# Projection stages of an attention kernel: both operand stacks of a tile are made ahead of the returns of turned heads, and products stand between a batch's last turns

## What is computed

```python
xn = _rms_norm(x, g_norm) * (1.0 + scale) + shift
qkv = (xn @ W_qkv).reshape(b, n, 3, h, d)          # 16 heads of 32
q = _rms_norm(q, g_q)
k = _rms_norm(k, g_k)
logits = jnp.einsum('bhqd,bhkd->bhqk', q, k) * d ** (-0.5)
attn = jax.nn.softmax(logits, axis=-1)
o = jnp.einsum('bhqk,bhkd->bhqd', attn, v)
return o + o @ W_out                               # o with its heads side by side
```

## Time and profile before

| | us |
|---|---|
| median of 3 runs | 2251.61 |
| lowest, highest | 2249.65, 2253.29 |
| the profiled execution | 2247.79 |
| its span in the trace | 2246.0 |
| busy PE, DVE, ACT, POOL | 2129.1, 1630.1, 1293.8, 527.2 |
| projection stage of batch 0 (first product to first score) | 60.3 |
| the same of batch 1 | 64.8 |
| the same of batch 3 | 71.6 |
| from 745 us to the end: the GRU and what goes with it | 1501 |

### The profile page before, as it was taken

The page is one execution under the profiler, slowest core; times in us unless marked ns, Lnnn a source line. Parts: engine busy times, 40 slices in busy tenths (PEclk is TensorE's granted clock), DMA queues, the critical chain, the costliest instruction groups (busy, mean ns, idle before and its releaser), DMA issues.

```text
span 2246.0 us, 135671 instructions
## 1 busy us (share of the span) xinstructions
PE 2129.1 (95%) x57232; PEld 1830.8 (82%) x57232; DVE 1630.1 (73%) x6269; ACT 1293.8 (58%) x5763; POOL 527.2 (23%) x2255
## 2 busy tenths in 40 slices
PE   5768999999989999999999999999999999999998
PEld 3654555645545899999999999999999999999997
DVE  7987967878678487777677776667766666766665
ACT  6765947758568345555556655555555545555553
POOL 2002121021120222332233322222222222222221
PEclk8559999999999999999999999999999999999999
DMA  5000000010010000000000000000000000000000
GB/s 208 3 2 1 1 1 1 1 57 1 1 57 1 22 5 5 5 1 1 1 1 1 1 11 1 1 11 1 1 11 1 1 1 10 1 1 11 13 9 14
DMA packets 8410, 26.49 MB, mean 12 GB/s; under 512 B 1028, under 2 KB 1352, under 8 KB 7880
## 3 DMA queue, kind: packets, MB, share of 16 engines
q1 hardware_dynamic: 7712, 23.07, 2.8%
q10 hardware_dynamic: 424, 0.07, 0.0%
HBM read 18.94 MB, written 4.19 MB: 10 GB/s over the span
## 4 chain that ended last, share of the span: by engine, by line
PE 80%; DVE 12%; ACT 4%; issue 2%; DMA 1%; POOL 0%; SPq 0%; DVEq 0%; POOLq 0%; ACTq 0%
PE psum L2257 54%; PE psum L2218 8%; PE psum L2005 3%; PE psum L1926 3%; PE psum L1968 2%; PE psum L2023 2%; PE psum L2103 2%; PE psum L1989 2%; DVE region_cols L1232 2%; DVE region_cols L1248 2%; DVE top L1425 2%; ACT region_rows L786 1%; PE psum L1945 1%; DMA region_cols<-in_L_cond_W_emb_dram 1%; PE psum L1902 1%
## 5 line engine op out<-in xcount | busy, mean ns | idle before, releaser
L2257 PE MATMUL psum<-partsA,region_w_hh 128*128 128x40 f16 x24576 | 855.3, 179 | 10.4 <-issue 4.8
L2257 PE MATMUL psum<-partsB,region_w_hh 128*128 128x40 f16 x24576 | 853.3, 179 | 0.6 <-issue 0.5
L2257 PEld LDWEIGHTS psum<-partsA,region_w_hh 128*128 128x128 f16 x24576 | 758.7, 96 | 37.1 <-issue 11.2
L2257 PEld LDWEIGHTS psum<-partsB,region_w_hh 128*128 128x128 f16 x24576 | 724.1, 96 | 1.1 <-issue 0.5
L599 POOL TENSOR_TENSOR region_w_b<-region_w_b 128x16 f32<-128x16 f32 x1022 | 245.3, 240 | 1078.4 <-DVE region_w_b L1751 1078.4
L1725 DVE TENSOR_REDUCE psum<-psum 128x8 f32<-128x32 f32 x1024 | 201.7, 197 | 198.6 <-PE psum L2257 187.7
L1061 ACT ACTIVATE mixA<-psum 128x8 f32<-128x8 f32 x512 | 95.3, 186 | 428.3 <-DVE psum L1725 428.3
L1075 ACT ACTIVATE region_w_b<-psum 128x8 f32<-128x8 f32 x1024 | 190.0, 186 | 144.0 <-DVE psum L1740 86.9
L601 POOL COPY region_work<-region_w_b 128x8 f32<-128x8 f32 x1024 | 230.9, 225 | 2.2 <-DVE region_w_b L1751 2.2
L1751 DVE TENSOR_TENSOR_SCAN region_w_b<-giveB,region_w_b 128x40 f32<-128x40 f32 x512 | 123.8, 242 | 129.0 <-ACT region_w_b L1075 129.0
L1732 DVE TENSOR_REDUCE psum<-psum 128x8 f32<-128x32 f32 x1024 | 191.1, 187 | 0.7 <-PE psum L2257 0.6
(11 more groups left out here) (265 smaller groups left out, 2820.9 us busy)
## 6 DMA issues: line engine op xcount, KB each, us to landing
region_rows<-in_x_dram SPq DMA_DIRECT2D x4, 1024.0 KB, 11.1
region_w_a<-in_L_cond_W_qkv_dram SPq DMA_DIRECT2D x1, 3072.0 KB, 23.4
region_w_hh<-in_L_cond_W_hh_dram SPq DMA_DIRECT2D x4, 768.0 KB, 6.3
region_w_a<-in_L_cond_W_ih_dram SPq DMA_DIRECT2D x1, 3072.0 KB, 9.9
out_dram<-region_w_b SPq DMA_DIRECT2D x12, 256.0 KB, 2.2
region_cols<-in_L_cond_W_emb_dram SPq DMA_DIRECT2D x1, 2048.0 KB, 19.5
region_cond<-in_cond_dram SPq DMA_DIRECT2D x1, 1024.0 KB, 11.0
region_w_a<-in_L_cond_W_out_dram SPq DMA_DIRECT2D x1, 1024.0 KB, 21.5
```

Of the source, the lines that this page charges most:

```text
L2257: made = e.matmul(k.slots(bank)[:, :, ch, :, 0:2], k.w16[:, 2 * read + c, part, NC * "rzn".index(g) + 2 * half + ch], k.parts[read][:, c]. ...
```

## The change

On ACT and DVE the order within a tile is changed. Both stacks of tile t - 1 are made one after the other. Then the keys of tile t - 2 are returned, tile t is taken (squares, reduction, roots), and only then are the queries of tile t - 1 returned. On DVE the normalising now stands at the end of `dve_take_projected`, ahead of the values. At a batch's end, the return of tile 2's keys stands behind both stacks of tile 3. On PE the order of the projections stays. Only between the turns of tile 3's queries and keys there stand now two matmuls, of output product 3 or, in batch 0, of the last values, for which `pe_project` got an argument for the input chunks. In batches 1 to 3 the other two matmuls of product 3 stand one before the first and one before the second pair of scores.

```diff
 def act_attention
     for t in range(1, NT):
+        act_stack(e, k, b, t - 1, 0)
+        act_stack(e, k, b, t - 1, 1)
         if t > 1:
             act_turn_stack(e, k, b, t - 2, 1)
-        act_stack(e, k, b, t - 1, 0)
+        act_take_projected(e, k, b, t)
         act_turn_stack(e, k, b, t - 1, 0)
-        act_stack(e, k, b, t - 1, 1)
-        act_take_projected(e, k, b, t)
...
-    act_turn_stack(e, k, b, NT - 2, 1)
     act_stack(e, k, b, NT - 1, 0)
     act_stack(e, k, b, NT - 1, 1)
+    act_turn_stack(e, k, b, NT - 2, 1)
...
 def dve_take_projected
     e.tensor_reduce(k.head_power[:, t], k.sq_qk, AX.X, ALU.add).then_inc(s["head_power"], 1)
-    if values_in_turn(b, t):
-        dve_values(e, k, b, t)
...
     e.reciprocal(k.head_power[:, t], k.head_power[:, t]).then_inc(s["head_power"], 1)
+    dve_norm_heads(e, k, b, t)
+    if values_in_turn(b, t):
+        dve_values(e, k, b, t)
...
 def dve_attention
     for t in range(1, NT):
+        dve_stack(e, k, b, t - 1, 0)
+        dve_stack(e, k, b, t - 1, 1)
+        if b == 0 and t == 1:
+            dve_mask_taken(e, k, b + 1)
         if t > 1:
             dve_turn_stack(e, k, b, t - 2, 1)
-        dve_norm_heads(e, k, b, t - 1)
-        dve_stack(e, k, b, t - 1, 0)
-        if b == 0 and t == 1:
-            dve_mask_taken(e, k, b + 1)
+        dve_take_projected(e, k, b, t)
         dve_turn_stack(e, k, b, t - 1, 0)
-        dve_stack(e, k, b, t - 1, 1)
-        dve_take_projected(e, k, b, t)
...
-    dve_turn_stack(e, k, b, NT - 2, 1)
-    dve_norm_heads(e, k, b, NT - 1)
     dve_stack(e, k, b, NT - 1, 0)
     dve_stack(e, k, b, NT - 1, 1)
     if b:
+        dve_turn_stack(e, k, b, NT - 2, 1)
         dve_out_adds(e, k, b - 1, (0, 1))
+        dve_turn_stack(e, k, b, NT - 1, 0)
+        dve_out_adds(e, k, b - 1, (2,))
     else:
         dve_values(e, k, b, NT - 2)
+        dve_turn_stack(e, k, b, NT - 2, 1)
+        dve_turn_stack(e, k, b, NT - 1, 0)
         dve_values(e, k, b, NT - 1)
-    dve_turn_stack(e, k, b, NT - 1, 0)
     dve_turn_stack(e, k, b, NT - 1, 1)
-    if b:
-        dve_out_adds(e, k, b - 1, (2,))
...
 def pe_attention
     if b:
         pe_out_matmuls(e, k, b - 1, (1, 2))
     else:
-        pe_project(e, k, b, NT - 1, (2,))
+        pe_project(e, k, b, NT - 1, (2,), range(0, 2))
     pe_turn_stack(e, k, b, NT - 1, 0)
+    if b:
+        pe_out_matmuls(e, k, b - 1, (3,), range(0, 2))
+    else:
+        pe_project(e, k, b, NT - 1, (2,), range(2, NC))
     pe_turn_stack(e, k, b, NT - 1, 1)
     if b:
-        pe_out_matmuls(e, k, b - 1, (3,), range(0, 2))
+        pe_out_matmuls(e, k, b - 1, (3,), range(2, 3))
     pe_scores(e, k, b, 0)
     if b:
-        pe_out_matmuls(e, k, b - 1, (3,), range(2, NC))
+        pe_out_matmuls(e, k, b - 1, (3,), range(3, NC))
```

More of the change, by code:

```diff
@@ L1904, in pe_norm_rows, with pe_project @@
     made.then_inc(s["normed_turned"], 1)
-def pe_project(e, k, b, t, outputs):
+def pe_project(e, k, b, t, outputs, cs=range(NC)):
     s = k.sem
@@ L1911, in pe_project @@
         bank = 3 * (t % 2) + i
-        if t == 0:
+        if cs[0]:
+            pass
+        elif t == 0:
             e.wait_ge(s["x_normed"], NC * (b + 1))
@@ L1924, in pe_project @@
             e.wait_ge(s["values"], n - 1)
-        for c in range(NC):
+        for c in cs:
             made = e.matmul(k.bank(bank, D), k.xnT[:, c, t * P:(t + 1) * P], k.w_qkv[:, c, i * D:(i + 1) * D],
                             start=(c == 0), stop=(c == NC - 1))
-        made.then_inc(s["projected"], 1)
+        if cs[-1] == NC - 1:
+            made.then_inc(s["projected"], 1)
 def pe_turn_stack(e, k, b, t, i):
```

## The result

The changed kernel takes 2242.5 us (median of 6 runs, 2239.0 to 2246.2), the kernel before beside it 2251.8 us (6 runs, 2249.7 to 2253.3). The ratio is 0.9960 with a 95% interval of 0.9947 to 0.9973: 9.3 us less. The forecast was 2236.8 us, 14.8 less. The time lies in the range (2232 to 2243), near its upper end, and the direction was right; 5.5 us of the forecast gain didn't come. The profiled execution took 2243.18 us with a span of 2241.5 (before: 2247.79 and 2246.0).

What follows compares the result with a forecast made beforehand. PE bounds the kernel, and only its waits in the four projection stages could move. Batch 0 -6.9, batches 1 and 2 +0.2 each and batch 3 -8.3 sum to -14.8 us: 2251.6 becomes 2236.8 us, range 2232 to 2243.

Steps and rivals of the forecast that it cites:

- The bounds of the terms: Ranges of the batch terms' gains; their ends together were -19.3 and -10.5 us, that is 2232.3 and 2241.1 us.
- Batch 3, -8.3 forecast: Batch 3's projection: 9.5 us of waits and slow clock go, 1.6 return, and 0.4 is gained at its end.
- the ring: DVE's sequence from one tile's reduction to the next in batch 3: 17.3 us before, 12.9 forecast, against PE's 12.3.
- Batch 0, -6.9 forecast: Batch 0's projection: PE's loss of 11.1 us falls to 4.2; bounds of -5.4 and -8.4.
- 4.2 us of waits left: Batch 0 under the new order: waits of 0.6, 0.8, 0.1, 0.7, 1.1 and, before the first score, 1.0 us.
- Batches 1 and 2, +0.2 forecast each: Their projections: later returns cost 0.6 us, the batch end gains 0.4; bounds of -0.7 and +1.0 each.
- the price of the first pairs: Batches 1 and 2, tiles 0 and 1: pairs beside POOL end about 3 us later than free ones.
- The strict reading: Each of four pair instructions waits out a POOL instruction of about 1.3 us: 5.1 us instead of 3, total 2241.0.
- the 3.4 that the prediction goes on with: Upper end of PE's waits for returned stacks in batches 1 and 2: 2.0 us become 2.5 to 3.4.
- The clock rival: A new wait in batch 0 or 3 lets the clock fall, 1.7 and 2.9 us return: 2241.4 us; chance 8%.
- the forecast's own case: The four stages shorten by 14.8 us in all, to 2236.8 us; chance 80%.
- The end of a batch, -0.4 each: Batches 1 to 3: one product less before a score brings the second pair of scores 0.4 us sooner.

Runs made afterwards that it cites:

- e7_norm_alone: Kernel before with only DVE's normalising moved behind the take of a tile's keys; 2247.4 us, ratio 0.9982 to the kernel before.
- e8_order_alone: Changed kernel with only the normalising put back at the start of the next tile; 2242.3 us, ratio 0.9969 to the kernel before.
- e4_pe_end_old: Changed kernel with PE's old order at a batch's end; 2241.4 us, ratio 0.9966 to the kernel before.
- e3_first_return: Changed kernel with tile 0's queries returned ahead of DVE's take and ACT's root in batches 0 to 2; 2234.3 us, ratio 0.9934 to before.
- e2_adds_late: Changed kernel with POOL's four output additions moved from tile 0 to tile 2; 2243.4 us, ratio 0.9969 to the kernel before.
- e5_keep_late: Changed kernel with POOL's copies of kept weights in batch 3 moved from the tiles into the softmax part; 2242.6 us, ratio 0.9960 to before.
- after_again: Changed kernel unaltered, run again on another chip; 2239.4 us, ratio 0.9947 to the kernel before.
- e1_old12: Changed kernel with the old order of ACT and DVE in batches 1 and 2 only; 2234.3 us, ratio 0.9935 to the kernel before.
- e9_halves: Changed kernel with several edits combined, kept-weight copies in batch 3's softmax part, each cut into two halves; 2224.9 us, ratio 0.9890 to before.

## Why the prediction was right, and where its size was wrong

The direction and the range held, the range in part by luck. The bounds of the terms ended at 2241.1 us. The measured 2242.5 is in the range only by the width that was added for scatter and for a fall of the clock in other batches. Of the terms only batch 3's stayed within its bounds. By the profiles the stages gained 6.3 us, not 14.8.

*Batch 3, -8.3 forecast, -7.5 measured* (to the second pair of scores, 74.7 to 67.2 us). The step held in its mechanism: no low part keeps PE waiting, no clock fall, the waits sit at second halves of turns. One term was too small. The pair beside the copies is 3.81 us, not 3.2, so the ring is 13.49, not 12.9, and PE waits 0.99 and 1.05 us in the two tiles with weights, 2.0 in all where I had 1.6. I had also spread this over five turns, where it is two. The other 0.4 us I can't place. That the normalising carries the gain, which a reader of the ring may think, is wrong alone (e7_norm_alone) and right on top of the order (e8_order_alone).

*Batch 0, -6.9 forecast, -4.7 measured.* I had found 4.2 us of waits left (the six terms add up to 4.3, as those of the loss before do to 11.2 and not 11.1; the difference stays 6.9). The listed ones alone come to 4.9. 0.85 us of the miss is PE's split of the last product, which I priced as a cover and not as something taken from ahead of another turn (e4_pe_end_old). About 0.9 is the return of tile 0's queries behind the take (54.6 us in e3_first_return), where I had 0.6 and 0.8. The rest, some 0.4 us, I can't place.

*Batches 1 and 2, +0.2 forecast each, with bounds of -0.7 and +1.0; +2.6 and +3.3 measured to the second pair.* This is the step that failed. The place was right (tile 0 and 1, waits for returned stacks), and so was the price of the first pairs: 2.34 + 3.20 us against twice 1.29 is 3.0 us later, as forecast. The strict reading of the Trainium skill (SBUF — State Buffer, section "SBUF: two separate sides") had given 5.1 for these pairs, and this the trace doesn't bear out: what fails is that each of the four waits out a whole instruction of POOL. But I left the scaling out of the chain, though the earlier trace rows had it at 0.74 us. It waits for POOL's addition, ACT's root waits for it, and ACT's return waits behind the root: 2.0 us where I had 1.1. e2_adds_late, where the scaling is free, shows the 1.1. DVE's return, 1.6 us, lies in the 1.4 to 2.0 that I had. (These terms add up to 2.5 to 3.1 us of waits and not to the 3.4 that the prediction goes on with; 3.6 were measured.) Without a fall of the clock the step is worth 0.9 us instead of 0.2 (batch 2 of e5_keep_late, 68.8 us to the second pair against 67.9 before). The rest, 1.7 us in batch 1 and 2.4 in batch 2, comes with the fall of the clock.

*The clock rival* was right in kind and wrong in place, and the forecast's own case had put the clock at nothing in batches 1 and 2. It named batches 0 and 3 and was held back by "the clock fell only after 3.7 and 4.5". It fell in batches 1 and 2, after 2.0 and 1.6. One execution of e5_keep_late shows the price, since the clock fell in its batch 1 and not in its batch 2. The two windows:

```profile
293.28:361.22 67.94, 64.33 (x259) 31.71 (x259) 50.24 (x78) 30.78 (x48) 17.18 (x12) 0.97 0.00 0
439.51:505.75 66.24, 62.63 (x260) 31.12 (x260) 50.23 (x78) 30.66 (x48) 17.18 (x12) 1.00 0.12 48
```

And PE's rows in its batch 2, which answer to those of batch 1 above:

```profile
467.22 0.61 PE L1947 MATMUL psum<-ident,region_rows 128*128 128x128 f16 x8 [2.02 <-ACT region_scratch L770]
469.42 0.62 PE L1947 MATMUL psum<-ident,region_rows 128*128 128x128 f16 x8 [1.59 <-DVE region_scratch L1405]
469.88 7.09 PE L1927 MATMUL psum<-region_w_a,region_work 128*128 128x512 f32 x16
```

The waits are the same, 7.09 us stand against 8.78, and the window is 1.70 us shorter.

*The end of a batch, -0.4 each.* Right in size, with 0.5, 0.5 and 0.3 us measured (e4_pe_end_old). In batch 0 the same edit costs 0.85.

*The sum and the median.* The four stages moved by -4.7, +2.6, +3.3 and -7.5, together -6.3, or -6.9 in after_again (-4.8, +2.6, +2.6, -7.4). The medians moved by 9.3. The profiled execution of before lies 4 us below the median of its runs, that of the changed kernel 0.7 above, so the pair of profiles shows only 4.6 us. The remaining 2 to 3 us I can't place in any one profile. Without them the time would lie above the range, so here too the number has had luck. The recurrence was said to keep its 1501 us. It does within a scatter that doesn't follow the edits, none of which touches it: the window from its first gate product to the end is 1501.8 us here, 1498.2 in e1_old12 and 1503.9 in e5_keep_late. By the count of matmuls done, a fall of the clock near 945 us, which some executions have, makes about 1 us of this in the changed kernel and 2.3 in e5_keep_late, and up to 3.5 us lie in the last eighth of the steps. What causes the latter is open.

## What to carry to other kernels

Price a small operation of VectorE beside GpSimd by what is left of the GpSimd instruction that it meets, not by its own size, and then follow who is queued behind it on the other engines: here 0.17 us became 1.1, a wait of PE grew by the difference, and the stage by 1.3. Where such an instruction can't be moved out of the way, cut it in pieces: moved whole it took its cost along, and halved it cost 2.0 us less in the profile. A wait that is taken away is worth measuring together with its neighbours, since two cures worth 1.3 us each gave 3.8 together, and in batch 3 one half of this change was worth nothing without the other.

## What the runs showed of the hardware

*A short operation waits until the GpSimd instruction that it meets has ended.* Three places show the same end. The first is the scaling in batch 3 of e5_keep_late:

```profile
605.10 1.22 DVE L1364 TENSOR_SCALAR head_power<-head_power 128x32 f32<-128x32 f32 x1
...
600.41 5.88 POOL L568 TENSOR_TENSOR region_cols<-region_cols,region_cond 128x512 f32<-128x512 f32 x4
```

It ends at 606.32 us, POOL's additions at 606.29. The others are the negative maxima, at 668.55 with the copy, and in e9_halves at 656.91 with the first half (656.89). Not every operation waits. Copies of DVE out of PSUM beside them keep their 0.68 us, and the reduction out of PSUM its 1.2. In batch 1 of the changed kernel the reciprocal at 321.10 us takes 0.35 us in the midst of POOL's additions, as it does without them, and the reduction of the squares at 318.45 us keeps its 1.21. The Trainium skill (SBUF — State Buffer, section "SBUF: two separate sides") says that the pair of ports shared by DVE and GpSimd is an exclusive lock, held for a whole instruction. The three ends agree with that within 0.03 us.

*The clock falls or not for the same waits.* With products of 16 matmuls behind the wait, the clock fell in batch 1 and stayed in batch 2 of one execution after 2.0 and 1.6 us (e5_keep_late), after one wait of 2.1 (e8_order_alone, 8.63 against 7.09 us) and after 1.1 and 1.2 (e2_adds_late, 8.66 us in batch 1 against 7.09 in batch 2). Batch 0 shows it between executions: after waits of 0.67 and 1.24 us eight matmuls take 5.07 us in e1_old12, and after 0.69 and 1.24 they take 3.65 in the changed kernel, whose batch 0 is the same code (5.01 in e2_adds_late, after 0.68 and 1.24). That is most of the 56.6 against 55.5 us of the table. In the kernel before, waits of up to 0.9 us in batch 1 went without a fall. So in this kernel a pair of waits of about 1 us each has to be given a chance of costing 1 to 2 us more, and between 1.2 and 2.1 us no length of wait in these runs separates the two outcomes. What decides is open. The times go with the mean clock: the six runs of the changed kernel have mean granted clocks of 0.966 to 0.971, the lowest with 2246.2 us and the highest with 2239.0.
